# Two attention layers and an MLP on one core: token blocks evacuated and split by VectorE alone, value copies of layer 1 ahead of the first shift

## The chip, the cores and the metric

The kernel runs on one core of one Trainium2 chip, as a single launch. The metric is device time in microseconds (us) of that core. The time before is the median of three runs.

## What is computed

The reference is two cross-attention layers over 16 batches of 256 tokens with 512 features, all in float32. Layer 0 is a perceiver-style layer (keys are the 256 context tokens and the 256 query tokens themselves) with an RMS norm and an MLP behind it; layer 1 attends from the result of layer 0 to the layer-normed context.

```python
# layer 0: latents = x (the query tokens), x = ctx_2048
h = jnp.concatenate([x, latents], axis=1)                  # 512 keys
q = (latents @ q_w + q_b).reshape(b, k_len, 16, 32)
kv = (h @ kv_w + kv_b).reshape(b, 512, 16, 32, 2)
attn = softmax(where(full_mask, einsum(q, k) / 32, -inf))
out = rmsnorm(einsum(attn, v) @ out_w + out_b + latents, postnorm_w)
x1 = gelu(out @ mlp_w1 + mlp_b1) @ mlp_w2 + mlp_b2 + latents
# layer 1: hidden_states = x1, audio_kv = ctx_2048
a = layer_norm(audio_kv)                                   # 256 keys
Q, K, V = hidden_states @ Wq.T, a @ Wk.T, a @ Wv.T         # 16 heads of 32
out = softmax(where(mask, Q K^T * 32 ** -0.5, -inf)) V
result = hidden_states + tanh(gate) * (out @ Wo.T)
```

## The kernel before

`build` runs three stages one after another: `attention_layer` with `layer=0`, `mlp`, and `attention_layer` with `layer=1`. The change is in `attention_layer` alone, which both layers share; `first` is true in layer 0. The precision of float32 is kept by splitting each operand of a matmul into a high and a low part (a "high" is the value copied to the type fp32r, a "low" is the rest, value minus high), and `product` (L60 to L67) makes three matmuls of the parts.

**The software pipeline.** A step of the outer loop, `iteration(p, a, ...)`, works on two batches at once: it projects batch `p` (its "items") and does the attention of batch `a = p - 1`. The same function stands once for each engine (SyncE for the DMAs, GpSimd, ScalarE, VectorE, TensorE), each with its own written-out order; semaphores tie them together. Batches 2 and later run with `a >= 1`: 14 such steps in each layer. The step with `a = 0` has its own distribution of work (`STEPS_AT_FIRST`), and a last step has no batch `p`.

**Items.** For batch `p` items 0 to 3 (`k < NT`, the "token blocks") are the transposes of the 512 token rows, 128 features at a time: `item` on TensorE transposes four 128x128 tiles (L994) into one of two PSUM banks, `item_ps[k % 2]`. ScalarE's `high(b, k)` then copies the bank to `hT[0]` as fp32r (L535), and VectorE's `low(b, k)` writes bank minus high to `hT[1]` (L762). Item `k` may not start on TensorE before the low of item `k - 2` is done (`low_done`), since there are two banks. Items 4 and later are the projections to keys and queries. In layer 0 their highs are L545 and L549 and their lows L769 and L774; in layer 1 they are L540 and L765, L766. In layer 0 there are 10 items, in layer 1 there are 8.

**The first pass.** The softmax of batch `a` is done twice over the scores. The first pass finds the maximum and the sum of each row. It has 32 steps in layer 0 and 16 in layer 1. A step is a score matmul on TensorE (`scores`, L1069, into a ring of four PSUM banks, `RING = 4`), a negated maximum on VectorE (`step_max`, L787) and an exponential with its sum on ScalarE (`step_sum`, L558; in layer 1 two of 256 columns). `scores(a, k)` waits for `step_sum(a, k - 4)`, and ScalarE and VectorE handle steps strictly in order. After half the steps VectorE's `make_shift(a, 0)` (L795 to L801) collects the maxima and the reciprocals of the sums, TensorE turns them (`turn_shift`, L1078), ScalarE copies them (L564) and a DMA puts them into the rows of `stack` that the second pass reads. The second pass (`shifted`, L1102, with `exps`, L578, and `weigh`, L1117) needs all sums: its second block waits for the last one.

**The slots.** The order is given by `SLOT`: one "share" slot, in layer 0 two "v" slots, then a slot for each of items 0 to 6. `STEPS_IN_SLOT` says how many first-pass steps belong to each slot. In layer 0 four steps run ahead of the first slot, and slots 0 to 9 take 2, 4, 4, 2, 1, 2, 1, 4, 4, 4 steps; the token blocks are slots 3 to 6, and `AFTER_T` = `TURN_SLOT` = 7. In layer 1 slots 0 to 7 take 2, 0, 2, 2, 2, 3, 3, 2 steps; the token blocks are slots 1 to 4, and `AFTER_T` = `TURN_SLOT` = 5. Value projections (`v_share`, `v_item`) fill TensorE between them; those banks are emptied by `copy_v`, on VectorE (L865) except for two of the four in layer 0, which are ScalarE's (L593). A token block's high may overwrite `hT[0]` only after the value projection has read it (`v_shared`, `v_done`).

**VectorE's order in a slot**, before: the first maximum of the slot, the low of this slot's token block, `make_shift`, the low of the previous slot's projection item, in layer 1 at `AFTER_T` the two value copies, then the other maxima. Layer 0 also has the squares and scaling of the RMS norm of batch `a - 1` in slots 1 and 3 (L840, L849) and its weighing in slot 9 (L856). **ScalarE's order**: in a slot with a token block, the high of it, then the sums of the slot before. **SyncE** issues the loads of the next tokens once item 3 is done (L311, L312), the shift rows (L392) and the stack (L318). GpSimd does part of the layer norm of the next batch during the second pass (L459 to L471).

Of the kernel before, what the change touches and what calls it, by code (L numbers as in the profile page):

```python
# [25 lines left out]
ACT = mybir.ActivationFunctionType  # L26
# [6 lines left out]
FB = D // P  # L33
# [44 lines left out]
def attention_layer(nc, layer, query_src, key_src, mask_src, weights, vectors, residual_src,  # L78
# [42 lines left out]
    AHEAD = RING if first else 0  # L121

    STEPS_AT_FIRST = [0, 0, 4, 4, 4, 4, 4, 4, 4, 4] if first else [0, 0, 2, 3, 3, 3, 3, 2]
    STEPS_IN_SLOT = [2, 4, 4, 2, 1, 2, 1, 4, 4, 4] if first else [2, 0, 2, 2, 2, 3, 3, 2]
    AFTER_T = SLOT.index(("item", NT))
    V_AHEAD = 1 if first else 2
    TURN_SLOT = AFTER_T
# [13 lines left out]
    with ctx:  # L141
# [365 lines left out]
        def _(act):  # L507
# [16 lines left out]
            def high(b, k):  # L524

                act.wait_ge(item_done, ITEMS * b + k + 1)
                ps, done = item_ps[k % 2], ITEMS * b + k + 1
                if k < NT:

                    if not isinstance(b, int) or b > 0:  # L530
                        if k < FB - 1:
                            act.wait_ge(v_shared, (FB - 1) * (b - 1) + k + 1)
                        else:
                            act.wait_ge(v_done, KB * b)
                    n = act.activation(hT[0][:, k, :], ps[:, :], ACT.Copy)  # L535
                elif not first:
                    g = k - NT

                    at_least(act, stack_loaded[g // GROUPS], 16 * STACK_DMAS * b)
                    n = act.activation(qk[:, g, :].rearrange("p (n s) -> p n s", s=S)[:, 0:4:3, :],  # L540
                                       ps[:, :].rearrange("p (n s) -> p n s", s=S), ACT.Copy)
                elif k < NT + NK:
                    g = k - NT
                    at_least(act, stack_loaded[g // GROUPS], 16 * STACK_DMAS * b)
                    n = act.activation(qk[:, g, K_HIGH], ps[:, 0:KEYS], ACT.Identity, bias=bk[:, g:g + 1])  # L545
                else:
                    for i in range(2):
                        g = 2 * (k - NT - NK) + i
                        n = act.activation(qk[:, g, Q_HIGH], ps[:, S * i:S * (i + 1)], ACT.Identity, bias=bq[:, g:g + 1])  # L549
                n.then_inc(high_done, 1)  # L550
# [102 lines left out]
            def iteration(p, a):  # L653
                for slot in range(SLOTS + 1):
# [2 lines left out]
                    if kind == "item" and n >= NT:  # L657
                        high(p, n)

                    kind, n = kind_of(slot, p, a)  # L660
                    if kind == "item" and n < NT:
                        high(p, n)
                    if a is not None:
                        if TURN_SLOT == slot - 1:
                            copy_shift(a, 0)
# [20 lines left out]
            for kind, n in FIRST:  # L686
                if kind == "split":
                    split_high(n)
                else:
                    if n == NT:  # L690
                        vectors_ready()
                    high(0, n)
# [7 lines left out]
        def _(dve):  # L700
# [48 lines left out]
            def layer_norm(b):  # L749

                dve.wait_ge(ln_rstd_done, b + 1)
                for t in range(QT):
                    n = dve.tensor_scalar(tokens[:, QT + t, :], tokens[:, QT + t, :], stat[:, t, 0:1],
                                          stat[:, t, 2:3], ALU.subtract, ALU.mult)
                n.then_inc(ln_step, 1)

            def low(b, k):

# [108 lines left out]
            def iteration(p, a, prev):  # L867
                for slot in range(SLOTS + 1):
                    steps = steps_of(slot, a) if a is not None and slot < SLOTS else []
                    kind, n = kind_of(slot, p, a)  # L870
                    for k in steps[:1]:
                        step_max(a, k)
                    if kind == "item" and n < NT:
                        low(p, n)
                    if a is not None and TURN_SLOT == slot:
                        make_shift(a, 0)
                    if a is not None and slot == SLOTS:
# [1 line left out]
                    kind, n = kind_of(slot - 1, p, a)  # L879
                    if kind == "item" and n >= NT:  # L880
                        low(p, n)
                    if not first and a is not None and slot == AFTER_T:
                        for t in range(KB):
                            copy_v(a, t)
                    for k in steps[1:]:
                        step_max(a, k)
                        if first and prev is not None and slot == NORM_SLOT + 1 and k < steps[-1]:
# [39 lines left out]
            for kind, n in FIRST:  # L927
# [13 lines left out]
                else:  # L941
                    if n == NT:
                        if first:
                            make_mask()
                        vectors_ready()
                    low(0, n)
            iteration(1, 0, None)
            with dve.Fori(2, B - 1) as i:
# [651 lines left out]
```

## Time and profile before

| | |
|---|---|
| median of three runs | 2507.28 us (2504.75 to 2508.92) |
| the profiled execution | 2504.85 us, span 2502.7 us |
| TensorE busy | 2371.9 us, 95% |
| ScalarE busy | 1454.3 us, 58% |
| VectorE busy | 1211.8 us, 48% |
| layer 0, steps in the steady state | 63.2 us each |
| layer 1, steps in the steady state | 42.3 us each |
| granted TensorE clock, mean | 0.973 |

The profile is of one execution. Busy times are sums of the durations of instructions; times on a timeline are microseconds from the start of the span. A duration is longer than the distance to the next instruction on the same engine when there is no wait between them, as instructions overlap at their ends. In square brackets is the time that an engine stood idle before an instruction, and what released it. The granted clock is a share of full speed: 1.0 is 2.4 GHz and 0.5 is 1.2 GHz.

### The profile page before, as it was taken

The numbers are of one execution on the slowest core, as the hardware profiler recorded it, in microseconds if no ns is written. First come the engines' busy times: TensorE is split into PE (matmuls) and PEld (weight loads), VectorE is DVE, ScalarE is ACT, GpSimd is POOL, SyncE is SP. The second block draws the span as 40 slices with busy tenths as digits, with TensorE's granted clock in tenths as the row PEclk, the third lists the DMA queues.
The fourth block names the chain that finished last, engine by engine and source line by source line (L and its number), as shares of the span: only waits on it lengthen the run. The fifth ranks groups of instructions, "written<-read, shape, count | busy, mean of one in ns | idle before, by whom it ended". The sixth has DMA issues, their size and how long they took to land. (4 is left out here: it accounts for less than half of the span.)

```text
span 2502.7 us, 43888 instructions
## 1 busy us (share of the span) xinstructions
PE 2371.9 (95%) x14656; PEld 1933.0 (77%) x14656; DVE 1211.8 (48%) x2382; ACT 1454.3 (58%) x3386; POOL 232.1 (9%) x260
## 2 busy tenths in 40 slices
PE   6999999999999999989999999999889999999998
PEld 5677777777777777668888888888678787777886
DVE  4455566566665666542122212211465666656564
ACT  3777777777777777743222222222277676767676
POOL 2000000000000000010000000000211212121210
PEclk9899999999999999889999999999899999999998
DMA  6244444444444443441011001102253535454443
GB/s 174 77 108 110 109 108 107 108 108 108 108 108 108 107 108 92 129 147 51 1 50 50 18 32 50 50 0 84 92 143 97 144 110 135 118 131 123 119 110 84
DMA packets 148186, 239.00 MB, mean 95 GB/s; under 512 B 25600, under 2 KB 59680, under 8 KB 148144
## 3 DMA queue, kind: packets, MB, share of 16 engines
q1 hardware_dynamic: 140944, 228.62, 33.8%
q10 hardware_dynamic: 7200, 9.84, 1.7%
q8 instruction: 24, 0.39, 0.1%
q14 instruction: 18, 0.15, 0.0%
HBM read 86.28 MB, written 25.21 MB: 45 GB/s over the span
## 5 line engine op out<-in xcount | busy, mean ns | idle before, releaser
L558 ACT ACTIVATE l_score_ps<-l_score_ps,l_neg_max 128x512 f32<-128x512 f32 (+1 forms) x1024 | 567.9, 565 | 186.9 <-DVE l_neg_max L787 186.9
L787 DVE TENSOR_REDUCE l_neg_max<-l_score_ps 128x1 f32<-128x512 f32 (+1 forms) x768 | 499.7, 685 | 81.2 <-PE l_score_ps L1069 77.7
L578 ACT ACTIVATE l_probs<-l_score_ps 128x1024 f32<-128x1024 f32 x384 | 382.2, 1017 | 80.2 <-PE l_score_ps L1102 78.1
L1434 ACT ACTIVATE mlp_hidden<-mlp_hidden_ps,mlp_b_col 128x512 f32<-128x512 f32 x128 | 88.3, 690 | 496.7 <-PE mlp_hidden_ps L67 496.7
L1069 PE MATMUL l_score_ps<-l_stack 97*128 97x512 f32 (+1 forms) x1024 | 315.1, 376 | 55.4 <-ACT l_score_ps L558 42.6
L1469 DVE TENSOR_TENSOR mlp_hidden_l<-mlp_hidden,mlp_hidden_h 128x512 fp32r<-128x512 f32 x128 | 92.4, 722 | 520.2 <-ACT mlp_hidden_h L1436 520.2
L1069 PEld LDWEIGHTS l_score_ps<-l_stack 97*128 97x128 f32 x1024 | 180.7, 200 | 106.0 <-ACT l_score_ps L558 77.7
L1102 PEld LDWEIGHTS l_score_ps<-l_stack 99*128 99x128 f32 x1536 | 213.2, 193 | 59.5 <-ACT l_score_ps L558 18.4
L1102 PE MATMUL l_score_ps<-l_stack 99*128 99x256 f32 x1536 | 244.8, 292 | 15.0 <-ACT l_score_ps L558 14.0
L558 ACT ACTIVATION_READ_ACCUMULATOR l_score_ps<-l_score_ps,l_neg_max 128x1 f32 x1024 | 223.0, 218 | 0.0
L65 PE MATMUL mlp_hidden_ps<-mlp_norm_h,mlp_w_l 128*128 128x512 f32 x512 | 200.5, 392 | 6.4 <-DVE mlp_norm_l L1464 6.4
L66 PE MATMUL mlp_hidden_ps<-mlp_norm_l,mlp_w_h 128*128 128x512 f32 x512 | 200.3, 391 | 0.0
L67 PE MATMUL mlp_hidden_ps<-mlp_norm_h,mlp_w_h 128*128 128x512 f32 x512 | 200.1, 391 | 0.0
L65 PE MATMUL mlp_sum_ps<-mlp_w_h,mlp_hidden_l 128*128 128x512 f32 x512 | 199.2, 389 | 0.0
L66 PE MATMUL mlp_sum_ps<-mlp_w_l,mlp_hidden_h 128*128 128x512 f32 x512 | 199.2, 389 | 0.0
L67 PE MATMUL mlp_sum_ps<-mlp_w_h,mlp_hidden_h 128*128 128x512 f32 x512 | 199.2, 389 | 0.0
L65 PE MATMUL l_item_ps<-l_hT_h,l_wk_l 128*128 128x512 f32 (+1 forms) x512 | 179.0, 350 | 9.6 <-DVE l_wk_l L717 5.6
L1117 PE MATMUL l_o_ps<-l_probs,l_v 128*32 128x256 f32 x3072 | 187.6, 384 | 0.0
L66 PE MATMUL l_item_ps<-l_hT_l,l_wk_h 128*128 128x512 f32 (+1 forms) x512 | 177.7, 347 | 0.0
L67 PE MATMUL l_item_ps<-l_hT_h,l_wk_h 128*128 128x512 f32 (+1 forms) x512 | 176.5, 345 | 0.0
L65 PE MATMUL l_item_ps<-l_hT_h,l_wq_l 128*128 128x256 f32 x512 | 151.2, 295 | 2.4 <-issue 1.0
L535 ACT ACTIVATE l_hT_h<-l_item_ps 128x512 fp32r<-128x512 f32 x128 | 77.1, 603 | 126.1 <-PE l_item_ps L994 123.3
(136 smaller groups left out, 4306.2 us busy)
## 6 DMA issues: line engine op xcount, KB each, us to landing
l_stack<-room SPq DMA_DIRECT2D x256, 192.0 KB
l_stack<-l_qk SPq DMA_DIRECT2D x196, 128.0 KB
l_stack<-room SPq DMA_DIRECT2D x128, 128.0 KB
l_stack<-l_qk SPq DMA_DIRECT2D x226, 64.0 KB
l_tokens<-in_x SPq DMA_DIRECT2D x16, 512.0 KB, 3.4
l_tokens<-in_ctx SPq DMA_DIRECT2D x16, 512.0 KB, 4.2
l_stack<-room SPq DMA_DIRECT2D x128, 64.0 KB
l_rows<-in_x SPq DMA_DIRECT2D x16, 512.0 KB, 3.3
```

Source lines behind the costliest of these rows:

```text
L65: pe.matmul(out, left_l, right_h, start=start, stop=False)
L66: pe.matmul(out, left_h, right_l, start=False, stop=False)
L67: return pe.matmul(out, left_h, right_h, start=False, stop=stop)
L535: n = act.activation(hT[0][:, k, :], ps[:, :], ACT.Copy)
L558: m = act.activation(e, e, ACT.Exp, bias=neg_max[:, q, h:h + 1], accum_out=row_sum[:, q, h:h + 1])
L578: act.activation(probs[:, s % PROBS, :].rearrange("p (a b) -> p a b", a=2), score_ps[:, 2 * (s % 2):2 * (s % 2) + 2, :], ACT.Exp).then_inc ...
L787: dve.tensor_reduce(out, bank, AXIS_X, ALU.max, negate=True).then_inc(max_done, 1)
L1069: m = pe.matmul(out, stack[0:ROWS_MAX, h, P * q:P * (q + 1)], stack[0:ROWS_MAX, h, K_COLS], start=True, stop=True)
L1102: n = pe.matmul(score_ps[:, 2 * (s % 2) + j // 2, S * (j % 2):S * (j % 2 + 1)], stack[0:ROWS_ALL, h, S + P * kb:S + P * (kb + 1)], stack[0 ...
L1117: n = pe.matmul(o_ps[g % 2][to, 0:S], v[:, kb, DH * h:DH * (h + 1)], probs[:, s % PROBS, S * j:S * (j + 1)], start=(kb == 0), stop=(kb == ...
L1434: act.activation(hidden[:, m % HBUF, :], hidden_ps[m % 4][:, :], ACT.Gelu_apprx_tanh, bias=b1_col[:, m:m + 1])
L1469: dve.tensor_tensor(hidden_p[1][:, m % HBUF, :], hidden[:, m % HBUF, :], f32(hidden_p[0][:, m % HBUF, :]), ALU.subtract).then_inc(hidden_l ...
```

## The change

Four things change in `attention_layer`, for both layers. The high of a token block is made by VectorE (`token_high`), directly ahead of its low, and ScalarE's `high` is no longer called for token blocks, neither in the steps nor at the start (`FIRST`). On VectorE the high and the low of a token block now stand ahead of the slot's first maximum. In layer 1 the two value copies stand ahead of the maximum and `make_shift` of slot `AFTER_T`, where they stood behind `make_shift`. In layer 1 slots 1 and 3 take 1 and 1 first-pass steps where they took 0 and 2.

```diff
-    STEPS_IN_SLOT = [2, 4, 4, 2, 1, 2, 1, 4, 4, 4] if first else [2, 0, 2, 2, 2, 3, 3, 2]
+    STEPS_IN_SLOT = [2, 4, 4, 2, 1, 2, 1, 4, 4, 4] if first else [2, 1, 2, 1, 2, 3, 3, 2]
...
                 act.wait_ge(item_done, ITEMS * b + k + 1)
                 ps, done = item_ps[k % 2], ITEMS * b + k + 1
-                if k < NT:
-
-                    if not isinstance(b, int) or b > 0:
-                        if k < FB - 1:
-                            act.wait_ge(v_shared, (FB - 1) * (b - 1) + k + 1)
-                        else:
-                            act.wait_ge(v_done, KB * b)
-                    n = act.activation(hT[0][:, k, :], ps[:, :], ACT.Copy)
-                elif not first:
+                if not first:
...
-                    kind, n = kind_of(slot, p, a)
-                    if kind == "item" and n < NT:
-                        high(p, n)
...
                 if kind == "split":
                     split_high(n)
-                else:
+                elif n >= NT:
...
+            def token_high(b, k):
+
+                dve.wait_ge(item_done, ITEMS * b + k + 1)
+                if not isinstance(b, int) or b > 0:
+                    if k < FB - 1:
+                        dve.wait_ge(v_shared, (FB - 1) * (b - 1) + k + 1)
+                    else:
+                        dve.wait_ge(v_done, KB * b)
+                dve.tensor_copy(hT[0][:, k, :], item_ps[k % 2][:, :]).then_inc(high_done, 1)
...
                     kind, n = kind_of(slot, p, a)
+                    if kind == "item" and n < NT:
+                        token_high(p, n)
+                        low(p, n)
+                    if not first and a is not None and slot == AFTER_T:
+                        for t in range(KB):
+                            copy_v(a, t)
                     for k in steps[:1]:
                         step_max(a, k)
-                    if kind == "item" and n < NT:
-                        low(p, n)
                     if a is not None and TURN_SLOT == slot:
                         make_shift(a, 0)
...
                     if kind == "item" and n >= NT:
                         low(p, n)
-                    if not first and a is not None and slot == AFTER_T:
-                        for t in range(KB):
-                            copy_v(a, t)
...
+                    if n < NT:
+                        token_high(0, n)
                     low(0, n)
```

## Rows read from the trace of the kernel before

**Rows 1.** Page, busy time by engine over the whole span.

```profile
PE 2371.9 (95%) x14656; PEld 1933.0 (77%) x14656; DVE 1211.8 (48%) x2382; ACT 1454.3 (58%) x3386; POOL 232.1 (9%) x260
```

**Rows 2.** Stretches: length, then PE, PEld, DVE, ACT, POOL, granted clock, DMA share, GB/s.

```profile
137.00:960.00 823.00, 803.44 (x5519) 637.19 (x5518) 493.73 (x990) 622.51 (x1329) 49.24 (x65) 1.00 0.44 109
...
1866.00:2460.00 594.00, 558.04 (x4136) 472.81 (x4135) 362.80 (x790) 412.41 (x1232) 88.27 (x104) 0.96 0.46 123
...
457.00:461.50 4.50, 3.86 (x21) 2.69 (x20) 4.50 (x9) 4.24 (x12) 0.00 (x0) 1.00 0.09 5
461.50:466.00 4.50, 4.43 (x21) 3.24 (x20) 4.37 (x12) 4.50 (x13) 0.00 (x0) 1.00 0.60 228
...
2343.30:2349.80 6.50, 6.50 (x31) 6.49 (x32) 4.22 (x11) 4.69 (x21) 0.00 (x0) 0.51 0.21 80
```

**Rows 3.** Groups by line and shape: total busy us, mean ns, idle before.

```profile
L762 DVE TENSOR_TENSOR l_hT_l<-l_item_ps,l_hT_h 128x512 fp32r<-128x512 f32 x128 | 87.8, 687 | 31.3 <-ACT l_hT_h L535 29.2
L535 ACT ACTIVATE l_hT_h<-l_item_ps 128x512 fp32r<-128x512 f32 x128 | 77.1, 603 | 126.1 <-PE l_item_ps L994 123.3
...
L865 DVE COPY l_v<-l_item_ps 128x512 f32<-128x512 f32 x32 | 22.0, 687 | 4.0 <-PE l_item_ps L67 2.7
```

**Rows 4.** Timeline of VectorE, one step of layer 0.

```profile
446.12 3.08 DVE L787 TENSOR_REDUCE l_neg_max<-l_score_ps 128x1 f32<-128x512 f32 x5 [1.01 <-PE l_score_ps L1069]
...
454.98 0.68 DVE L787 TENSOR_REDUCE l_neg_max<-l_score_ps 128x1 f32<-128x512 f32 x1
456.01 0.69 DVE L762 TENSOR_TENSOR l_hT_l<-l_item_ps,l_hT_h 128x512 fp32r<-128x512 f32 x1 [0.35 <-ACT l_hT_h L535]
...
457.22 0.87 DVE L849 TENSOR_SCALAR l_rows<-l_rows,l_stat 128x512 f32<-128x512 f32 x2
...
462.20 0.68 DVE L787 TENSOR_REDUCE l_neg_max<-l_score_ps 128x1 f32<-128x512 f32 x1
462.79 0.17 DVE L795 CAST l_shift<-l_neg_max 128x16 fp32r<-128x16 f32 x1
462.87 0.25 DVE L796 RECIPROCAL l_inv_raw<-l_row_sum 128x16 f32<-128x16 f32 x1
463.15 0.17 DVE L798 CAST l_shift<-l_inv_raw 128x16 fp32r<-128x16 f32 x1
...
463.46 2.67 DVE L787 TENSOR_REDUCE l_neg_max<-l_score_ps 128x1 f32<-128x512 f32 x4
466.99 0.75 DVE L769 SCALAR_TENSOR_TENSOR room<-l_item_ps,l_bk,room 128x512 fp32r<-128x512 f32 x1 [0.86 <-ACT room L545]
```

**Rows 5.** Timeline of ScalarE, same step of layer 0.

```profile
466.20 0.75 ACT L545 ACTIVATE room<-l_item_ps,l_bk 128x512 fp32r<-128x512 f32 x1
```

**Rows 6.** Timeline of TensorE, same step of layer 0.

```profile
476.07 0.74 PE L1102 MATMUL l_score_ps<-l_stack 99*128 99x256 f32 x4 [0.71 <-ACT l_score_ps L558]
```

**Rows 7.** Timeline of VectorE, one step of layer 1.

```profile
2037.87 1.29 DVE L787 TENSOR_REDUCE l_neg_max<-l_score_ps 128x2 f32<-128x512 f32 x2
2039.62 0.69 DVE L762 TENSOR_TENSOR l_hT_l<-l_item_ps,l_hT_h 128x512 fp32r<-128x512 f32 x1 [0.46 <-ACT l_hT_h L535]
...
2049.68 0.17 DVE L795 CAST l_shift<-l_neg_max 128x16 fp32r<-128x16 f32 x1 [1.48 <-ACT l_score_ps L558]
...
2050.44 1.29 DVE L865 COPY l_v<-l_o_ps 128x512 f32<-128x512 f32 x2
2051.65 1.88 DVE L787 TENSOR_REDUCE l_neg_max<-l_score_ps 128x2 f32<-128x512 f32 x3
```

**Rows 8.** Timeline of ScalarE, same step of layer 1.

```profile
2052.36 0.45 ACT L558 ACTIVATE l_score_ps<-l_score_ps,l_neg_max 128x256 f32<-128x256 f32 x1 [1.81 <-DVE l_neg_max L787]
```

**Rows 9.** Timeline of TensorE, same step of layer 1.

```profile
2044.66 0.50 PE L1069 MATMUL l_score_ps<-l_stack 97*128 97x256 f32 x2 [0.76 <-ACT l_score_ps L558]
...
2046.96 0.50 PE L1069 MATMUL l_score_ps<-l_stack 97*128 97x256 f32 x2 [0.89 <-ACT l_score_ps L558]
...
2051.78 0.39 PE L1078 MATMUL l_o_ps<-ident,l_shift 128*32 128x128 f32 x2 [0.97 <-DVE l_v L865]
```

## The prediction

> **What bounds the kernel now.** I read the page first, then busy time by stretch, then the timelines of one repeated step of each layer. The page puts TensorE at 95% and VectorE at 48% [rows 1], so one would call VectorE cheap. That mean hides where the work lies. In the steady state of layer 0 VectorE is busy for 494 of 823 us, but the change puts its new work into the token blocks, and there it works 4.50 of 4.50 us and then 4.37 of 4.50, with ScalarE at 4.24 and 4.50 and TensorE at 3.86 and 4.43 [rows 2]. So three engines are near full at once, and which one ends the stretch last has to be walked. In layer 1 TensorE waits visibly in the token blocks, for sums made by ScalarE, 0.76 us at the first and 0.89 at the last of three waits, and 0.97 before the first shift is turned, there for the value copies [rows 9].
>
> **Price of the parts.** On ScalarE a token block's high takes 603 ns. On VectorE the nearest row is the value copy, also PSUM to SBUF, 128x512: 687 ns [rows 3]. Undisturbed neighbours on VectorE start closer together than they last: five maxima take 3.08 us, so 0.60 us from one start to the next [rows 4]. The low has to wait for the high ahead of it, so that overlap is lost there; the wait of one VectorE operation on another costs 0.03 us (reciprocal from 462.87, 0.25 long, next operation at 463.15) [rows 4]. So a high on VectorE adds 0.69 + 0.03 = 0.72 us per token block, 2.88 for the four. The bounds: two scalings of 128x512 take 0.87 us, one start 0.39 after the other [rows 4], though they read SBUF; that would make 0.39 + 0.12 = 0.51 per block. The slowest elementwise row of this shape, 0.75 against 0.69 [rows 4], makes 0.78. I take 0.72, as the value copy has source, shape and operation in common and only the output type differs. The Trainium skill (VectorE: DVE Perf Modes, "Why PSUM operands drop a tier") says that a float32 operand in PSUM keeps VectorE at one element per cycle where a copy inside SBUF can take two; the two rows agree with that, 687 ns from PSUM against a distance of 0.39 us in SBUF. ScalarE is freed of four times 0.6 us, and the handover of each block from ScalarE to VectorE goes.
>
> **Layer 0, one steady step.** On VectorE the stretch begins at 454.98, right behind the second value copy, and is unbroken to the first shift but for the wait for ScalarE's high at 456.01: the maximum ahead of it could have been followed at 455.58, so 0.43 us are lost. The maximum of slot 7 starts at 462.20 [rows 4]: 7.22 us for six maxima and four lows at 0.60, the scaling at 0.79 and this 0.43. After the change the 0.43 go and 2.88 come: 2.45 us later, so that maximum starts at 464.65 and the first shift at 465.25. The new waits of `token_high` don't stall, as each item is ready on TensorE before VectorE reaches it (item 0 is done 0.8 us before 454.98, and VectorE only gets later). Behind each of them stand the slot's maxima, for which ScalarE and then TensorE (ring of four banks) wait, so the lateness spreads. Maxima 20 to 24 follow 2.45 later. ScalarE has little to do meanwhile, but its sums can't be made before the maxima: the last sum ahead of item 4's high ends about 0.06 us behind its maximum plus three sums at 0.66, and this high moves from 466.20 [rows 5] to 468.65, again 2.45. The low of item 4 waits for that high, as it does now (0.86 us idle, at 466.99 [rows 4]), and the maxima behind it wait for the low. From there the two engines hand each other the work to the last sum. TensorE alone would be late by only about 1.8 us (its step for item 4 waits for sums 17 and 19), but the second block of the second pass waits for the last sum already now, 0.71 us idle at 476.07 [rows 6], so it takes the full 2.45. Behind that, TensorE runs without a gap to speak of, so nothing gives it back. 14 steps: 14 x 2.45 = **+34.3 us**. With the bounds of the price, 14 x (4 x 0.51 - 0.43) = +22.5 and 14 x (4 x 0.78 - 0.43) = +37.7.
>
> **Layer 1, one steady step.** VectorE from its first maximum at 2037.87 [rows 7]: eight maxima (4.8 us), four highs with lows (4 x 1.32 = 5.28), two value copies (1.2), the maximum of slot 5 (0.6) brings the first shift to 2049.75. Its other condition, sum 7, ends two sums of 0.90 us behind maximum 6, which ends at 2047.4, so at 2049.3, earlier than now, since no high stands between the sums. So the shift is made at the same time as now (2049.68 [rows 7]), but the value copies are behind it no more: TensorE turns it when it is made, 0.76 us on (2049.68 to 2050.44 [rows 7]), at about 2050.5 instead of 2051.78 [rows 9], and the next maximum starts at 2050.50 instead of 2051.65 [rows 7]. ScalarE waits for that maximum now (1.81 us idle at 2052.36 [rows 8]) and starts at 2051.23. All that follows hangs on this chain of maximum, sum, high and low: -1.13 us per step, 14 x 1.13 = **-15.8 us**. The spreading of steps costs nothing by itself: one score step of 0.24 us moves past 1.5 us of value matmuls on TensorE. With a price of 0.51 the step gains up to 1.13 + 0.84 = 1.97, with 0.78 it gains 0.89.
>
> **The rest.** In the last step of layer 1 there are no items, and the two copies no longer stand between the first and second half: -1.2. At the start of layer 1 four blocks run through VectorE alone, which then has a long reduction: +0.9. At the start of layer 0 the four blocks end before the weights are there: 0. The first step of layer 0 has VectorE waiting for TensorE between its blocks: 0, between -3 and +2. SyncE's queue is passed by nothing: item 3 is done within 0.4 us of now, and the token loads it releases have the rest of the step; the stack of the second half is needed about 2 us earlier in layer 1 (step 8 at 2045.0 instead of 2046.96 [rows 9]), and if it landed only at 2046 TensorE would still be ready before sum 6 lets it go on at 2048.4. GpSimd is not touched.
>
> **Sum.** 34.3 - 15.8 - 1.2 + 0.9 = +18.2 us. On the profiled execution, 2504.85 us, that is 2523.0; the median of the runs lies 2.4 higher, so 2525.5 there. A measurement here tells apart about 0.2%, some 5 us.
>
> **Rivals.**
> (a) *The lateness in layer 0 is hidden, the gain in layer 1 stays.* For it: half of VectorE's time is idle, and ScalarE, freed of 2 us per step, might catch up. Then 2507.3 - 15.8 - 0.3 = 2491. Against it: windows without idle time, and the wait at 476.07 that is ScalarE's already. It decides if the last sum of a step comes no later, relative to the step's start, than now. 0.12.
> (b) *The copy is cheap.* The net is 14 x (8x - 4.44) for a price of x us per block: +18 at 0.72, zero at 0.555, -5 at 0.51. So the sign turns at a price of 0.555, and at the lower end the time is 2502. 0.08.
> (c) *TensorE's clock.* In three of the 14 steps of layer 1 the granted clock falls to 0.51, which is 1.2 GHz, for 6.5 us right behind the three waits of the token blocks [rows 2, 9]. After the change layer 0 has such a stretch: TensorE waits for the low of item 2 (about 1.3 us), then for sums 17, 18 and 19, where it is at full clock through the whole stage now [rows 2]. 6.5 us at half speed lose about 3.2 us of work there, of which 0.7 are cover. If all 14 steps had it, 14 x 2.5 = +35, time 2560; if a quarter had it, +9, 2534. Layer 1, with shorter waits, might lose its three: -4. 0.15 for 2533 or more. The Trainium skill (TensorE: Matmul & The Clock Gate, "HAM oscillation — how this bites in real kernels") describes such a loss, a clock that falls with the gaps between groups of matmuls; the rows agree that it fell behind gaps.
> The forecast, VectorE as the bound of layer 0's token blocks with a price near 0.72: 0.65, between 2512 and 2533.
>
> **Numbers.** 2525 us. The range takes in the bounds of the price (with 0.78: 14 x (8 x 0.78 - 4.44) = +25, so 2532), the lower prices down to near no change, and rival (c) with a third of the steps: 2508 to 2542. Left out below are rival (a) and most of (b), above the worse cases of (c). Slower by over 0.2%: forecast and (c), 0.80. Within: part of (b), 0.05. Faster: (a) and the rest of (b), 0.15.
>
> **What would show it.** Right: steps of layer 0 at 65.7 us instead of 63.2, with VectorE's maximum of slot 7 2.4 us later behind item 0, a wait of TensorE for that chain in its item 4, and about 2.4 us more between item 3 and the second pass; steps of layer 1 at 41.2 instead of 42.3, with the wait before the turned shift near 0.4; a high on VectorE of 0.69 us and its low 0.03 behind. Wrong: a copy under 0.6 us; no idle on TensorE in item 4 of layer 0; a granted clock under 1.0 in layer 0's steady state; or steps of layer 1 as long as now, which would mean that the shift was made later by as much as the copies cost.

## The result and the profile after

The changed kernel takes 2515.12 us (median of six runs, 2512.92 to 2516.38), the kernel before 2505.62 us in the six runs beside them (2503.83 to 2508.92): a ratio of 1.0036, with 95% interval 1.0023 to 1.0049. It is slower, by about half of what was forecast (+9.5 us instead of +18). The profiled execution of after took 2512.92 us, its span is 2511.1 us, 8.4 more than before.

The starts of item 0 on TensorE (L994 before, L996 after) cut both spans into the same pieces:

| piece (us) | before | after | difference | forecast |
|---|---|---|---|---|
| start, to item 0 of layer 0's first step | 60.22 | 61.15 | +0.93 | 0 |
| layer 0, first step (`a = 0`) | 76.88 | 70.30 | -6.58 | 0 |
| layer 0, the next 13 steps | 822.23 | 852.77 | +30.54 | +31.9 |
| 14th step, last step, MLP, to layer 1's first item | 837.22 | 839.41 | +2.19 | +2.4 |
| start of layer 1 | 24.76 | 26.44 | +1.68 | +0.9 |
| layer 1, first step | 45.61 | 46.76 | +1.15 | 0 |
| layer 1, the next 13 steps | 553.32 | 535.52 | -17.80 | -14.7 |
| 14th step and last step | 82.46 | 78.75 | -3.71 | -2.3 |
| span | 2502.70 | 2511.10 | +8.40 | +18.2 |

Two pieces stand out: a first step that gains 6.6 us where nothing was forecast, and layer 1, which gains 4.5 us more than forecast. First the page's busy times of after, against [rows 1].

```profile
PE 2366.8 (94%) x14656; PEld 1923.2 (77%) x14656; DVE 1286.0 (51%) x2510; ACT 1400.8 (56%) x3258; POOL 232.1 (9%) x260
```

VectorE has 128 instructions and 74 us more, ScalarE 128 fewer. The stretches of after, with the columns of [rows 2]: the first step of layer 0, its 13 steady steps, and the 13 of layer 1.

```profile
61.00:131.40 70.40, 67.32 (x428) 51.86 (x427) 44.02 (x84) 51.82 (x117) 3.80 (x5) 0.95 0.45 109
131.40:984.20 852.80, 810.94 (x5513) 642.41 (x5512) 526.60 (x1041) 599.93 (x1275) 49.21 (x65) 0.99 0.42 105
1896.80:2432.30 535.50, 508.32 (x3850) 425.45 (x3848) 366.10 (x794) 362.75 (x1092) 88.31 (x104) 1.00 0.48 129
```

The granted clock of layer 1 is 1.00, where [rows 2] has 0.96: none of its 14 steps behind the first has a fall of the clock any more, where before ten of the 14 had one (three long ones, in the steps that had more than the usual 42.3 us, and seven short ones at no cost). In layer 0 the clock is 0.99 and was 1.00: five of the 14 steps have a short fall (0.974 over the step), and they are as long as the others. The two groups of the token blocks in after, to be held against [rows 3]:

```profile
L754 DVE CAST l_hT_h<-l_item_ps 128x512 fp32r<-128x512 f32 x128 | 87.4, 682 | 11.2 <-PE l_item_ps L996 11.2
L761 DVE TENSOR_TENSOR l_hT_l<-l_item_ps,l_hT_h 128x512 fp32r<-128x512 f32 x128 | 88.5, 692 | 4.4
```

A high takes 682 ns, the value copy of [rows 3] took 687. VectorE in one steady step of layer 0 of after (item 0 starts at 459.42, in [rows 4] at 453.60, so 5.82 is to be taken off):

```profile
460.80 0.68 DVE L754 CAST l_hT_h<-l_item_ps 128x512 fp32r<-128x512 f32 x1
461.52 0.69 DVE L761 TENSOR_TENSOR l_hT_l<-l_item_ps,l_hT_h 128x512 fp32r<-128x512 f32 x1
462.12 1.28 DVE L786 TENSOR_REDUCE l_neg_max<-l_score_ps 128x1 f32<-128x512 f32 x2
463.32 0.87 DVE L848 TENSOR_SCALAR l_rows<-l_rows,l_stat 128x512 f32<-128x512 f32 x2
...
469.88 1.28 DVE L786 TENSOR_REDUCE l_neg_max<-l_score_ps 128x1 f32<-128x512 f32 x2
471.07 0.17 DVE L794 CAST l_shift<-l_neg_max 128x16 fp32r<-128x16 f32 x1
```

From the high at 460.80 to its low at 461.52 are the 0.72 us of the forecast, and nothing stalls until the shift. The shift is made 11.65 us behind item 0 (471.07 - 459.42), before it was 9.19 (462.79 - 453.60 [rows 4]): 2.46 later. TensorE in the same step:

```profile
465.57 0.66 PE L996 MATMUL l_item_ps<-ident,l_tokens 128*128 128x128 f32 x4 [0.70 <-DVE l_hT_l L761]
...
467.57 0.50 PE L1071 MATMUL l_score_ps<-l_stack 97*128 97x512 f32 x1 [1.10 <-DVE l_hT_l L761]
...
471.42 0.50 PE L1071 MATMUL l_score_ps<-l_stack 97*128 97x512 f32 x1 [0.41 <-ACT l_score_ps L550]
...
484.27 0.74 PE L1104 MATMUL l_score_ps<-l_stack 99*128 99x256 f32 x4 [1.26 <-ACT l_score_ps L550]
```

TensorE's waits for VectorE's lows are longer now, 0.70 and 1.10, where the same step before has 0.27 and 0.38:

```profile
459.35 0.66 PE L994 MATMUL l_item_ps<-ident,l_tokens 128*128 128x128 f32 x4 [0.27 <-DVE l_hT_l L762]
...
460.62 0.49 PE L1069 MATMUL l_score_ps<-l_stack 97*128 97x512 f32 x1 [0.38 <-DVE l_hT_l L762]
```

The wait for a sum (0.41) in item 4 is new, and the wait for the last sum that stood at 0.71 [rows 6] is 1.26. A step is 65.60 us long (forecast 65.7), all thirteen alike. VectorE in a step of layer 1 of after (item 0 at 2061.78):

```profile
2071.59 1.28 DVE L864 COPY l_v<-l_o_ps 128x512 f32<-128x512 f32 x2
2072.79 0.68 DVE L786 TENSOR_REDUCE l_neg_max<-l_score_ps 128x2 f32<-128x512 f32 x1
2073.39 0.17 DVE L794 CAST l_shift<-l_neg_max 128x16 fp32r<-128x16 f32 x1
2074.05 1.89 DVE L786 TENSOR_REDUCE l_neg_max<-l_score_ps 128x2 f32<-128x512 f32 x3
```

And TensorE and ScalarE there:

```profile
2068.80 0.48 PE L1071 MATMUL l_score_ps<-l_stack 97*128 97x256 f32 x2 [0.55 <-ACT l_score_ps L550]
...
2070.26 0.50 PE L1071 MATMUL l_score_ps<-l_stack 97*128 97x256 f32 x2 [0.27 <-ACT l_score_ps L550]
...
2072.19 0.50 PE L1071 MATMUL l_score_ps<-l_stack 97*128 97x256 f32 x2 [0.71 <-ACT l_score_ps L550]
...
2074.37 0.38 PE L1080 MATMUL l_o_ps<-ident,l_shift 128*32 128x128 f32 x2 [0.26 <-DVE l_shift L800]
```

```profile
2074.77 0.45 ACT L550 ACTIVATE l_score_ps<-l_score_ps,l_neg_max 128x256 f32<-128x256 f32 x1 [0.25 <-DVE l_neg_max L786]
```

The copies stand ahead of the shift, the shift is turned 12.59 us behind item 0 (before 13.58: 2051.78 [rows 9] less item 0 at 2038.20), and ScalarE's wait of 1.81 [rows 8] is 0.25. The three waits of the token blocks, 0.76, 0.41 and 0.89 before (the first and the last in [rows 9]), are now 0.55, 0.27 and 0.71. A step takes 41.17 us, where 42.33 was usual before and three steps had more (44.33, 43.41, and the fourteenth, whose end shows in no start of an item 0).

### The profile page after: what moved, and what is told of

Its sections match the earlier page's. It is cut to its first block and busy times, and to the rows that moved or that the text cites. A ratio compares the mean times of both kernels' runs of the same rounds, so it can differ in the third digit from the quotient of the medians.

```text
span 2511.1 us, 43776 instructions
## 1 busy us (share of the span) xinstructions
PE 2366.8 (94%) x14656; PEld 1923.2 (77%) x14656; DVE 1286.0 (51%) x2510; ACT 1400.8 (56%) x3258; POOL 232.1 (9%) x260
## 5 line engine op out<-in xcount | busy, mean ns | idle before, releaser
L786 DVE TENSOR_REDUCE l_neg_max<-l_score_ps 128x1 f32<-128x512 f32 (+1 forms) x768 | 491.8, 684 | 41.9 <-PE l_score_ps L1071 41.1
L1104 PE MATMUL l_score_ps<-l_stack 99*128 99x256 f32 x1536 | 244.7, 292 | 19.9 <-ACT l_score_ps L550 18.8
L550 ACT ACTIVATION_READ_ACCUMULATOR l_score_ps<-l_score_ps,l_neg_max 128x1 f32 x1024 | 207.0, 202 | 0.0
L66 PE MATMUL l_item_ps<-l_hT_l,l_wq_h 128*128 128x256 f32 x512 | 146.0, 285 | 0.0
```

The lines of the kernel that those rows point to most:

```text
L66: pe.matmul(out, left_h, right_l, start=False, stop=False)
L550: m = act.activation(e, e, ACT.Exp, bias=neg_max[:, q, h:h + 1], accum_out=row_sum[:, q, h:h + 1])
L786: dve.tensor_reduce(out, bank, AXIS_X, ALU.max, negate=True).then_inc(max_done, 1)
L1104: n = pe.matmul(score_ps[:, 2 * (s % 2) + j // 2, S * (j % 2):S * (j % 2 + 1)], stack[0:ROWS_ALL, h, S + P * kb:S + P * (kb + 1)], stack[0 ...
```

## The first step of layer 0: where the forecast missed

The forecast had VectorE "waiting for TensorE between its blocks: 0". ScalarE was not walked there. Its timeline in that step, before:

```profile
61.12 0.59 ACT L535 ACTIVATE l_hT_h<-l_item_ps 128x512 fp32r<-128x512 f32 x1
63.64 0.60 ACT L535 ACTIVATE l_hT_h<-l_item_ps 128x512 fp32r<-128x512 f32 x1 [1.93 <-PE l_item_ps L994]
64.14 0.66 ACT L558 ACTIVATE l_score_ps<-l_score_ps,l_neg_max 128x512 f32<-128x512 f32 x1
...
70.52 0.60 ACT L535 ACTIVATE l_hT_h<-l_item_ps 128x512 fp32r<-128x512 f32 x1 [3.61 <-PE l_item_ps L994]
```

VectorE and TensorE, before:

```profile
61.09 0.69 DVE L787 TENSOR_REDUCE l_neg_max<-l_score_ps 128x1 f32<-128x512 f32 x1
62.35 1.88 DVE L787 TENSOR_REDUCE l_neg_max<-l_score_ps 128x1 f32<-128x512 f32 x3
```

```profile
63.00 0.60 PE L994 MATMUL l_item_ps<-ident,l_tokens 128*128 128x128 f32 x4
64.96 0.49 PE L1069 MATMUL l_score_ps<-l_stack 97*128 97x512 f32 x1 [1.35 <-ACT l_score_ps L558]
...
71.84 0.50 PE L1069 MATMUL l_score_ps<-l_stack 97*128 97x512 f32 x1 [1.35 <-ACT l_score_ps L558]
...
76.84 0.79 PE L1069 MATMUL l_score_ps<-l_stack 97*128 97x512 f32 x1 [1.35 <-ACT l_score_ps L558]
```

A maximum was ready at 61.8, but its sum stood in ScalarE's order behind the high of the next item, and that item came from TensorE only at 63.6. So the sum started at 64.14, and TensorE, whose next score matmul waits for it (ring of four), stood for 1.35 us, and again at 71.84 and 76.84. In the steady step of [rows 4] nothing of the kind shows on TensorE: in the token blocks it waits only for lows there, and for no sum. Whether the other order would gain there too was not tried. After the change the sums no longer have a high in front of them. TensorE in the same step after:

```profile
63.92 0.60 PE L996 MATMUL l_item_ps<-ident,l_tokens 128*128 128x128 f32 x4
64.82 0.51 PE L1071 MATMUL l_score_ps<-l_stack 97*128 97x512 f32 x1 [0.31 <-ACT l_score_ps L550]
...
72.25 0.50 PE L1071 MATMUL l_score_ps<-l_stack 97*128 97x512 f32 x1 [0.77 <-ACT l_score_ps L550]
```

From item 0 to the first score matmul behind item 3 it was 16.62 us (60.22 to 76.84) and is 11.10 (61.15 to 72.25). The two stretches, before and after, with the columns of [rows 2]:

```profile
60.22:76.84 16.62, 11.88 (x41) 7.59 (x39) 10.17 (x17) 9.12 (x25) 0.00 (x0) 0.78 0.28 60
61.15:72.25 11.10, 9.20 (x41) 6.00 (x39) 10.99 (x19) 7.24 (x22) 0.00 (x0) 1.00 0.50 110
```

Of the 5.5 us, TensorE was idle for 2.8 (4.74 before, 1.90 after); the other 2.7 are the same 41 matmuls, busy for 11.88 us at a granted clock of 0.78 and for 9.20 at 1.00. So the waits themselves make about half of the gain, and the clock that was low among them the other half.

## Experiments

Medians, and the ratio to the kernel before in the runs beside them. The last columns are lengths between starts of item 0 in the profiled execution; where two lengths stand, both are usual, and the longer ones go with a fallen clock. `i_double` and `k_max_first` have two executions each, the others four to ten.

| label | median us | ratio (95%) | layer 0 first / steady | layer 1 steady |
|---|---|---|---|---|
| before | 2505.62 | 1 | 76.9 / 63.2 | 42.33 |
| after | 2515.12 | 1.0036 (1.0023 to 1.0049) | 70.3 / 65.6 | 41.17 |
| a_l0_old | 2488.27 | 0.9922 (0.9906 to 0.9939) | 77.4 / 63.2 | 41.16 |
| b_l0_first | 2482.30 | 0.9900 (0.9884 to 0.9917) | 71.7 / 63.2 | 41.17 |
| c_l1_old | 2534.85 | 1.0107 (1.0090 to 1.0124) | 71.7 / 65.6 | 42.36 |
| d_sums_first | 2501.91 | 0.9978 (0.9968 to 0.9988) | 71.2 / 63.2 | 42.35 |
| e_v_late | 2499.43 | 0.9962 (0.9948 to 0.9976) | 71.7 / 63.2 | 42.15 |
| f_steps_old | 2487.84 | 0.9920 (0.9903 to 0.9936) | 71.0 / 63.2 | 41.5 to 41.6 |
| g_v_only | 2491.80 | 0.9943 (0.9927 to 0.9959) | 71.8 / 63.2 | 41.05; 42.1, 43.3 |
| h_half | 2510.06 | 1.0006 (0.9992 to 1.0020) | 71.6 / 64.6 | 42.1, 43.3 |
| i_double | 2553.45 | 1.0188 (1.0144 to 1.0232) | 70.8 / 67.5 | 42.1, 43.3 |
| k_max_first | 2526.55 | 1.0081 (1.0060 to 1.0101) | 70.7 / 65.8, 67.3 | 41.16 |
| l_fill | 2480.64 | 0.9903 (0.9886 to 0.9919) | 71.6 / 63.2 | 41.03 |

**Layer by layer.** `a_l0_old` leaves layer 0 as before and keeps the whole change in layer 1. In it and in all that follow, a function `on_vector` says whose a token block's high is:

```diff
+        def on_vector(b, a, k):
+            at_first = isinstance(a, int) and a == 0
+            where = "start" if a is None else "first" if at_first else "steady"
+            return where in (() if first else ("start", "first", "steady"))
...
-                    if kind == "item" and n < NT:
+                    if kind == "item" and n < NT and on_vector(p, a, n):
                         token_high(p, n)
```

> Layer 0 as before (token blocks' highs on ScalarE everywhere), layer 1 with the whole change. My theory: the steady steps of layer 0 lose 2.35 us each to VectorE, the first step of layer 0 gains 6.6 us, and layer 1 gains. From the two profiles, layer 1 from its first item on takes 687.5 us after the change and 706.2 before, so this kernel should be 18.7 us faster than before, about 2487 us, with steps of 63.2 us in layer 0 and 41.2 us in layer 1. Rival, that the two layers are coupled through TensorE's clock or the alignment of loops: layer 1 gains less than 14 us.

It took 2488.27 us, as expected; in layer 1 none of the 14 steps behind the first has a fallen clock. `b_l0_first` also gives VectorE the highs of layer 0's first step (`("first",) if first else ...`).

> As a_l0_old, but in the one step of layer 0 with a = 0 the highs of the token blocks are on VectorE. My theory: it adds the gain of 6.6 us of that step, which came of ScalarE no longer standing in a high behind which the sums wait, so about 2480 us, the first step of layer 0 at 70.3 instead of 76.9 us. Rival, that the 6.6 us were TensorE's clock, that happened to fall less often in that profile: about 2487 us, step at 74 to 77 us.

It took 2482.30 us, and the first step falls from 77.4 to 71.7 us, where 70.3 was expected. `c_l1_old` is the counterpart: the change in layer 0 alone, layer 1 as before.

> The change in layer 0 alone, layer 1 as before. Theory: before plus 8.4 (the change) plus 18.7 (the gain of layer 1 given up), about 2533 us, with steps of 65.6 us in layer 0 and 42.3 in layer 1. If low-clock stretches of layer 1 are chance of its alignment, their number here is anything from 0 to 4; if the waits of the old layer 1 bring them, there are some again.

It took 2534.85 us, with layer 0 at 65.6 per step, layer 1 at 42.36, and the clock of layer 1 as before: ten of 14 steps have a fall, three of them a long one. Against the 2507.1 beside both, the two layers' parts are thus +27.8 (`c_l1_old`) and -18.8 us (`a_l0_old`), and their sum, +8.9, is what the whole change does (+9.5).

**Is the first step's gain in ScalarE's order?** `d_sums_first` is the kernel before, VectorE's work untouched, with two statements of ScalarE swapped in that one step:

```diff
+                    token = kind == "item" and n < NT and not on_vector(p, a, n)
+                    sums_first = first and isinstance(a, int) and a == 0
-                    if kind == "item" and n < NT:
+                    if token and not sums_first:
                         high(p, n)
...
                                 step_sum(a, k)
+                        if token and sums_first:
+                            high(p, n)
```

> The kernel before with one edit: in the step of layer 0 with a = 0, ScalarE makes the sums of the slot before ahead of the token block's high instead of behind it; all highs stay on ScalarE. If the first step's gain is ScalarE's order (it stood waiting in the high of a block that TensorE had not transposed while finished maxima waited for their sums), the step shrinks from 76.9 to about 71 us and the time falls by 5 to 7 us, to about 2500. If the gain came of moving the work to VectorE, nothing changes: 2506.

The step fell from 76.9 to 71.2 us and the time by 0.22% (interval 0.12 to 0.32%). The gain needs no work moved to VectorE: taking the high from the head of ScalarE's queue is enough. The granted clock of the step rises with it, from 0.89 to 0.95, as in after.

**What bounds layer 0's steady step?** Four loads of VectorE, and the length of the step for each. `h_half` gives two of the four highs to VectorE, `i_double` all four and a reduction of 128x512 between high and low whose result nobody reads (output as before).

```diff
-            return where in (("first",) if first else ())
+            return where in (("first", "steady") if first else ()) and (not first or where != "steady" or k >= 2)
```

```diff
                         token_high(p, n)
+                        if first and not isinstance(a, int):
+                            dve.tensor_reduce(stat[:, 0, 4 + n:5 + n], item_ps[n % 2][:, :], AXIS_X, ALU.max)
                         low(p, n)
```

> As g_v_only, but in the steady steps of layer 0 the highs of token blocks 2 and 3 are on VectorE and those of 0 and 1 on ScalarE. Theory, VectorE's chain bounds the token blocks one for one at 0.72 us per high: 63.2 + 1.44 = 64.6 us per step, against 65.6 with four, so 20 us more than g_v_only. Rival, that the loss is a fixed one, of the hand-over to TensorE in item 4: 65.3 us or more; rival that ScalarE bounds: 63.2.

> Layer 1 as in g_v_only, layer 0 with all highs of the steps on VectorE, and in 13 of its 14 steady steps a needless reduction of 512 columns between the high and the low of each token block. It fills the hand-over, so it adds 4 x (0.60 - 0.12) = 1.9 us to VectorE's chain. Theory, VectorE bounds the stretch one for one: steps of 67.5 us instead of 65.6. Rival, that VectorE's lateness is partly slack and 65.6 has another bound (ScalarE, TensorE's own waits): less than 66.6.

Layer 0's steps: 63.2, 64.6, 65.6 and 67.5 us for 0, 2 and 4 highs and for 4 with the extra reduction, as expected. Each us put on VectorE's chain lengthens the step by about as much (1.87 us for the last 1.9). In `i_double` the clock falls in all of these steps (0.95 to 0.975 over the step, 67.47 us for the shorter falls and up to 67.93 for the longer ones), in `h_half` in none. (`h_half` has 1.4 us for its two highs, not half of 2.4: the wait for ScalarE's first high, the 0.43 us of the forecast, is still paid in it.) `h_half` took 2510.06 us, where 2502 was expected (20 more than the 2482 expected of `g_v_only`), and `i_double` 2544 and 2562. Their layer 1 has the code of `g_v_only`, but 12 and 14 of its 14 steps have a fallen clock; that is taken up below.

**The order of maximum and high.** `k_max_first` is after with layer 0's first maximum of a slot ahead of high and low:

```diff
+                    for k in steps[:1] if first else ():
+                        step_max(a, k)
                     if kind == "item" and n < NT and on_vector(p, a, n):
                         token_high(p, n)
                         low(p, n)
...
-                    for k in steps[:1]:
+                    for k in steps[:1] if not first else ():
                         step_max(a, k)
```

> The changed kernel, but in layer 0 the slot's first maximum stands ahead of the high and low of the token block again. Theory: the length of VectorE's chain counts and not its order, so layer 0's steps stay at 65.6 us within 0.3 and the time at 2515. Rival, that the late maxima (sums 17 and 19 that TensorE waits for in item 4) make part of the loss: steps of 65.0 us or less, 2507 or less.

That missed: 2526.55 us, 11 more than after. Its first steady step takes 65.59 us, then the steps alternate between 65.8 and 67.3. Layer 0 behind its first step, columns as above:

```profile
131.40:1010.00 878.60, 837.49 (x5563) 665.91 (x5563) 544.66 (x1068) 616.15 (x1300) 49.31 (x65) 0.96 0.41 102
```

The granted clock is 0.96, in after 0.99. The one step at a full clock is as long as those of after, so no cost of the order by itself shows. All the others have a fall, a short one at 65.8 us and a long one at 67.3. TensorE's wait for the low of item 0 is 1.27 us here and 0.70 in after, the one behind it 1.10 in both. In after, falls in five steps cost nothing.

**What gains in layer 1?** `e_v_late` is `b_l0_first` with the value copies behind the shift again, `f_steps_old` is `b_l0_first` with the old numbers of steps per slot, and `g_v_only` has the value copies ahead and nothing else of the change in layer 1.

```diff
-                    if not first and a is not None and slot == AFTER_T:
-                        for t in range(KB):
-                            copy_v(a, t)
...
                     if kind == "item" and n >= NT:
                         low(p, n)
+                    if not first and a is not None and slot == AFTER_T:
+                        for t in range(KB):
+                            copy_v(a, t)
```

```diff
-    STEPS_IN_SLOT = [...] if first else [2, 1, 2, 1, 2, 3, 3, 2]
+    STEPS_IN_SLOT = [...] if first else [2, 0, 2, 2, 2, 3, 3, 2]
```

> As b_l0_first (layer 0: highs on VectorE in the first step only; layer 1: the whole change, steps of 41.17 us), but the two value copies of layer 1 stand behind the first shift again. Theory: VectorE reaches the shift 0.4 us earlier (then sum 7 holds it), the two copies of 1.2 us stand between the shift and the next maximum again, so that maximum comes 0.8 us later: steps of 41.9 to 42.0 us, about 2493 us. Rival, that freeing ScalarE of the highs makes the gain of layer 1: steps stay near 41.2, about 2482.

> As b_l0_first, but slots 1 and 3 of layer 1 take 0 and 2 first-pass steps again. Theory: VectorE's work to the first shift is the same and nearly unbroken, but it waits some 0.2 us for the transposes of block 1, as maximum 2 no longer fills that time: steps of 41.2 to 41.5 us, 2482 to 2487 us. Rival, that the spread is needed: 42 us or more.

> As b_l0_first in layer 0; layer 1 is that of before (highs on ScalarE, old steps) with one edit: the two value copies stand ahead of the maximum and the first shift of their slot. Theory: VectorE has 1.5 us to spare there while sums 6 and 7 are made, so the copies cost nothing and the next maximum comes 1.15 us earlier: steps of 41.2 us, about 2482 us, the whole gain without moving the highs. Rival, that the highs on VectorE are needed for it: steps of 42.3 us, about 2498. Low-clock steps, which the old layer 1 had three times in each of three profiles, may stay.

`e_v_late` loses 0.98 us per step, near all of the gain (at 2499.43 us it is 6 us above what was expected, its steps 0.2 us longer): without the new order of the copies the highs on VectorE, with the spread steps, are worth 0.15 to 0.2. `f_steps_old` loses 0.35 to 0.45; six of its 14 steps have a short fall of the clock, at no more than 0.1 us. In `g_v_only` the undisturbed step is 41.05 us, even a little shorter than in after: the copies alone give the whole length. Yet its time is 2491.8 and not 2482, and its ten runs spread over 21 us (2483.87 to 2505.28). In its profile the clock falls in seven of the 14 steps, which take 42.1 us with a short fall and 43.3 with a long one (the first of them 41.92). Stretches of an undisturbed and of a disturbed step of `g_v_only`, each cut at its waits in the token blocks and behind them:

```profile
2162.70:2165.10 2.40, 1.03 (x5) 0.62 (x5) 2.20 (x4) 2.40 (x11) 0.00 (x0) 1.00 0.72 212
2165.10:2168.80 3.70, 3.70 (x31) 3.67 (x32) 3.10 (x10) 3.58 (x16) 0.00 (x0) 1.00 0.38 146
2245.90:2248.20 2.30, 1.00 (x4) 0.59 (x4) 2.10 (x4) 2.30 (x10) 0.00 (x0) 1.00 0.65 213
2248.20:2253.90 5.70, 5.69 (x35) 5.67 (x36) 4.09 (x11) 5.18 (x23) 0.00 (x0) 0.70 0.25 98
```

TensorE in the disturbed one:

```profile
2245.90 0.50 PE L1094 MATMUL l_score_ps<-l_stack 97*128 97x256 f32 x2 [0.76 <-ACT l_score_ps L564]
2246.81 0.50 PE L1094 MATMUL l_score_ps<-l_stack 97*128 97x256 f32 x2 [0.41 <-ACT l_score_ps L564]
2248.21 0.52 PE L1094 MATMUL l_score_ps<-l_stack 97*128 97x256 f32 x2 [0.90 <-ACT l_score_ps L564]
...
2253.40 0.38 PE L1103 MATMUL l_o_ps<-ident,l_shift 128*32 128x128 f32 x2
```

TensorE waited 0.76, 0.41 and 0.90 us; then its matmuls of 256 columns start 0.21 us apart instead of 0.12, and the shift is turned 8.87 us behind item 3 (2244.53 to 2253.40), in the undisturbed step 7.39. The undisturbed step has the same three waits to 0.01 us. So these waits alone don't decide whether the clock falls.

**Are the waits the cause?** `l_fill` is `g_v_only` with item 3's transposes done three times in layer 1 (the same values into the same bank), which fills the first of the waits:

```diff
+                    for _ in range(3 if not first and a is not None and k == NT - 1 else 1):
                         for t in range(2 * QT):
                             n = pe.transpose(ps[:, P * t:P * (t + 1)], tokens[:, t, P * k:P * (k + 1)], ident[:, :])
```

> g_v_only with one addition: in layer 1 the four transposes of item 3 are done three times over on TensorE (same result), some 0.5 us of work that lies in its wait before step 6, as ScalarE copies that block 2 us later. If the falls of TensorE's clock in g_v_only (5 of 14 steps in its profile) come of the waits in the token blocks, there are fewer of them: 0 to 2 in 14, median about 2483 and a spread of 5 us instead of 21. If they don't depend on these waits, the count stays and the median stays at 2492. Undisturbed steps stay at 41.05 us.

```profile
2156.66 1.48 PE L1020 MATMUL l_item_ps<-ident,room 128*128 128x128 f32 x12
2158.02 0.50 PE L1095 MATMUL l_score_ps<-l_stack 97*128 97x256 f32 x2
2158.93 0.50 PE L1095 MATMUL l_score_ps<-l_stack 97*128 97x256 f32 x2 [0.41 <-ACT l_score_ps L564]
2160.33 0.50 PE L1095 MATMUL l_score_ps<-l_stack 97*128 97x256 f32 x2 [0.89 <-ACT l_score_ps L564]
```

The wait of 0.77 is gone, the other two are as they were, and the needless work delays nothing (41.03 us per undisturbed step). The clock falls in two steps of 14 instead of seven, the median is 2480.64 and the four runs lie within 5 us: 11 us faster than `g_v_only`, by adding work. All profiles together, for the 14 steps of layer 1 behind the first (waits of TensorE for sums in the token blocks, and steps with a granted clock under 1.00):

| kernels | the waits (us) | together | steps with a fall |
|---|---|---|---|
| before, `c_l1_old`, `d_sums_first` | 0.76, 0.41, 0.89 | 2.06 | 10, 10, 10 |
| `g_v_only`, `h_half`, `i_double` | 0.76, 0.41, 0.90 | 2.07 | 7, 12, 14 |
| `f_steps_old` | 0.41, 1.10, 0.35 | 1.86 | 6 |
| after, `a_l0_old`, `b_l0_first`, `e_v_late`, `k_max_first` | 0.55, 0.28, 0.71 | 1.54 | 0 in each |
| `l_fill` | 0.41, 0.89 | 1.30 | 2 |

With the long waits the clock falls in half of the steps or more, with the shorter ones in few or none. But three kernels with one and the same code in layer 1 have 7, 12 and 14, and `l_fill`, with the least waiting, still has two: the waits are shown to bear on it, and what else does is open. The Trainium skill (TensorE: Matmul & The Clock Gate, "A second HAM failure mode: psum-queue depth-cycling") tells of a clock that moves between its two levels because TensorE idles briefly between groups of matmuls; `g_v_only` and `l_fill` agree with it.

## Why the prediction was right and wrong

- **The bound of layer 0's token blocks, right.** VectorE's stretch without idle time set the pace, and ScalarE did not catch up: 2.46 us later at the shift, and four loads of VectorE that each came back on the step. Rival (a), the hidden lateness, fell with `c_l1_old` (+28 us).
- **The price of a high, right.** 0.72 us from high to low, where 0.72 was taken; rival (b) fell. (Its lower end was also reckoned too low: a gain of 1.97 us in layer 1 at 0.51 per block, though by the prediction's own walk sum 7, which ends at 2049.3, lets the shift come only 0.4 us earlier; that makes 1.6, and no gain in the total.) The usual step came 2.39 us longer (63.21 to 65.60) and not 2.45; the lateness of 2.46 at the shift is 2.38 at the second pass's second block (22.47 us behind item 0 before, 24.85 after). And the first of the 13 steps had been 63.64 us before, 0.43 over the others, and isn't now. Together 1.6 us of the error over 14 steps.
- **Layer 1's steady step, right in size and place.** 1.16 us were measured for 1.13 (42.33 to 41.17), and `e_v_late` shows that the order of the value copies brings it. "The spreading of steps costs nothing by itself" is a little off: beside highs on VectorE it gains 0.35 us or more.
- **The failed step: "The first step of layer 0 has VectorE waiting for TensorE between its blocks: 0, between -3 and +2."** It was -6.58, the largest part of the 10 us that the sum was off. The step looked at the engine that gets the work and not at the one that is rid of it; `d_sums_first` shows that ScalarE's order alone makes 5.7 of it: the step before stood three times for 1.35 us behind highs that waited for TensorE, and ran those blocks at a granted clock of 0.78. That `c_l1_old` and `b_l0_first` have 71.7 and after 70.3 is within what this step scatters over kernels that have it alike.
- **Layer 1's steps at a fallen clock** were named in rival (c) ("might lose its three: -4") and left out of the sum. They vanished: 3.1 us in the 13 steps (-17.80 against 13 x 1.13 = 14.7) and some 1.4 in the last ones. The reading was also short: the three steps are those with a long fall, and seven more had a short one that cost nothing. The highs on VectorE leave TensorE's step length about as it is (41.17 against 41.05 in `g_v_only`), but with the spread steps they shorten its waits from 0.76 and 0.89 to 0.55 and 0.71, and every kernel with these shorter waits kept its clock. `l_fill` shows that filling a wait helps; that the shorter waits are the whole reason is argued from the table and not shown. Rival (c)'s fall in layer 0 did come, in five of 14 steps (0.99 over the layer, which the prediction had named as a sign of being wrong), but cost nothing: those steps are as long as the others. `k_max_first` shows how near the loss was.
- **Starts.** +0.93, +1.68 and +1.15 us at the start of the layers and layer 1's first step were forecast at 0, 0.9 and 0. `c_l1_old` and `d_sums_first` have layer 1 as before and show 26.3 for its start and 47.4 to 47.5 for its first step, as much as after or more. So no effect of the change is shown in them. The start of layer 1 goes with the granted clock in it: 24.7 to 24.8 us at 0.93 (before, `h_half`), 26.0 to 26.4 at 0.80 to 0.82 (after, `a_l0_old` to `e_v_late`, `i_double`, `l_fill`), 25.5 to 25.7 between. The 47.4 us of the first step go with 0.89, but its 46.76 in after stand at 0.93, as the 45.61 before do, and that difference is left unexplained. Why the clock differs there from kernel to kernel was not found.

The error of the sum, 18.2 - 8.4 = 9.8 us, is thus 6.6 (first step), 4.5 (clock), 1.6 (steady step of layer 0), less 2.9 of starts.

What stays open: which of two steps with equal waits loses its clock; the profiled run of `g_v_only` has seven of each kind.

## What to carry to other kernels

Before moving an operation off an engine, walk the queue it leaves as well as the one it joins: a copy out of PSUM that waits for a late matmul holds back finished work behind it (1.35 us three times here), and two swapped statements give that back without touching the other engine. A mean load says nothing of a stretch: VectorE is at 48% over the span, but in a stretch in which it is never idle every microsecond added to it lengthened the step by about one, so look at the stretch that will take the work. And where two orders have the same undisturbed length, compare their waits on TensorE too: here a kernel with waits of 0.76, 0.41 and 0.90 us lost 11 us to its clock that a filled wait gave back. The kernels that win here (`b_l0_first`, `l_fill`, both about 1% faster than before) keep layer 0's highs on ScalarE but for its first step, and the value copies of layer 1 ahead of the shift.

## What was not expected of the hardware

- Three waits of 0.76, 0.41 and 0.90 us within 3 us are followed by a granted clock of 0.70 over 5.7 us in one step of `g_v_only` and of 1.00 in another; without the first of them (`l_fill`) two steps of 14 are hit instead of seven.
- A fall of the clock need not cost anything: seven steps of layer 1 before and five of layer 0 in after had one and were as long as the rest, while in `g_v_only` one takes about 1 us or more.
- Needless transposes of 0.9 us per step made a kernel 11 us faster and narrowed its runs from 21 to 5 us.
- A copy from PSUM takes ScalarE 603 ns [rows 3] and VectorE 682, so the engine that bounds layer 0's token blocks is also the slower one at this work.
